# A graph layer on one core: SyncE fetches a chunk's 128 rows in 14 turns instead of 16

## The reference

```
xn  = layernorm(x)
x   = x + gnn(xn, src, dst) + mix(xn)        # gnn: two SAGE layers, mix: linear attention + MLP
x   = x + ffn(layernorm(x))                  # each row goes to one of 8 experts

sage(x) = (segment_sum(x[src], dst) / max(count, 1)) @ Wl.T + b + x @ Wr.T
gnn     = sage2(relu(sage1(xn)))
```

## Time and profile before

| | |
|---|---|
| runs before | 2389.92, 2390.24, 2394.78 us; median 2390.24 us |
| profiled execution | 2393.41 us, of it a span of 2391.6 us |
| PE busy | 1915.2 us (80%) |
| POOL busy | 1650.4 us (69%) |
| DVE busy | 1152.5 us (48%) |
| ACT busy | 549.1 us (23%) |
| gathers L758 | 771 of layer 1 (737.5 us busy), 771 of layer 2 (731.2 us busy) |
| DMA engines | busy 35.4% with GpSimd's queue, 4.4% and 7.0% with the other two |

### The profile page before, as it was taken

The page is one execution under the profiler, slowest core; times in us unless marked ns, Lnnn a source line. Parts: engine busy times, 40 slices in busy tenths (PEclk is TensorE's granted clock), DMA queues, the critical chain, the costliest instruction groups (busy, mean ns, idle before and its releaser), DMA issues.

```text
span 2391.6 us, 54474 instructions
## 1 busy us (share of the span) xinstructions
PE 1915.2 (80%) x9589; PEld 1184.8 (50%) x9590; DVE 1152.5 (48%) x3201; ACT 549.1 (23%) x1242; POOL 1650.4 (69%) x1753
## 2 busy tenths in 40 slices
PE   3799999888688878786899999987665543689999
PEld 2456555555455555552455555443332211378887
DVE  8545554443577777774655545543332221342222
ACT  6434443333122222220122222211110000101111
POOL 6777777777777777757777777777777777164442
PEclk9999999999899999897899999998776655689999
DMA  7444444444444444434455454444444443455552
GB/s 218 137 131 130 133 131 128 128 127 127 134 138 136 129 140 140 143 100 143 150 163 161 153 164 152 152 153 142 129 131 120 117 120 108 149 184 169 166 163 82
DMA packets 166333, 336.14 MB, mean 141 GB/s; under 512 B 41189, under 2 KB 101063, under 8 KB 166181
## 3 DMA queue, kind: packets, MB, share of 16 engines
q0 software_dynamic: 84768, 245.32, 35.4%
q10 hardware_dynamic: 42630, 58.35, 7.0%
q1 hardware_dynamic: 38786, 31.12, 4.4%
HBM read 273.98 MB, written 58.72 MB: 139 GB/s over the span
## 4 chain that ended last, share of the span: by engine, by line
PE 40%; POOL 24%; issue 14%; DVE 11%; DMA 3%; DVEq 3%; ACT 1%; POOLq 1%; ACTq 1%; SPq 1%
POOL big L758 23%; PE bank L572 14%; PE bank L1790 8%; PE bank L1555 7%; PE bank L1778 2%; PE bank L1561 2%; DMA mbuf<-qT_d 2%; PE bank L1711 1%; DVEq L506 1%; PE bank L1585 1%; PE bank L1580 1%; DVE m_s L1085 1%; POOL big L768 1%; DVE bank L1079 1%; DMA big<-hh_d,edges 1%
## 5 line engine op out<-in xcount | busy, mean ns | idle before, releaser
L758 POOL DMA_INDIRECT big<-xh_d,edges x771 | 737.5, 957 | 245.0 <-issue 227.4
L758 POOL DMA_INDIRECT big<-hh_d,edges x771 | 731.2, 948 | 242.7 <-issue 228.0
L1555 PE MATMUL bank<-big,S 128*128 x1960 | 585.2, 424 | 225.5 <-SPq L629 186.3
L957 DVE SCALAR_TENSOR_TENSOR S<-edges,tv,bank 128x512 f16<-128x512 f32 x490 | 365.5, 747 | 439.8 <-PE bank L1555 253.8
L1555 PEld LDWEIGHTS bank<-big,S 128*128 128x128 f16 x1960 | 203.0, 104 | 511.2 <-issue 368.4
L1553 PE MATMUL bank<-ones,S 128*128 128x1 f16 x980 | 166.0, 169 | 40.7 <-SPq L629 30.6
L572 PE MATMUL bank<-turned,x1T 128*128 128x512 f32 x392 | 195.2, 620 | 0.0
L779 POOL DMA_INDIRECT out_dram<-big,node_s x56 | 56.8, 1014 | 145.5 <-DVE big L1290 136.7
L1483 ACT ACTIVATE x1T<-bank 128x256 f32<-128x256 f32 x49 | 18.8, 383 | 503.9 <-PE bank L1561 494.4
L1553 PEld LDWEIGHTS bank<-ones,S 128*128 128x128 f16 x980 | 95.7, 98 | 54.2 <-SPq L629 37.7
L1290 DVE SCALAR_TENSOR_TENSOR big<-bank,prob_s,res 128x256 f32<-128x256 f32 x56 | 27.1, 484 | 180.1 <-PE bank L1792 180.1
(11 more groups left out here) (229 smaller groups left out, 2903.6 us busy)
## 6 DMA issues: line engine op xcount, KB each, us to landing
hx_d<-mbuf ACTq DMA_DIRECT2D x49, 512.0 KB
big<-xh_d,edges POOLq DMA_INDIRECT x771
big<-hh_d,edges POOLq DMA_INDIRECT x771
st<-xh_d SPq DMA_DIRECT2D x768, 1.0 KB
ik<-hh_d SPq DMA_DIRECT2D x768, 1.0 KB
ik<-xh_d SPq DMA_DIRECT2D x640, 1.0 KB
st<-hh_d SPq DMA_DIRECT2D x640, 1.0 KB
big<-in_fwd_dram SPq DMA_DIRECT2D x8, 1024.0 KB, 12.3
```

Source lines behind the costliest of these rows:

```text
L758: e.indirect_dma_start(GS[layer][:, r, n % SC, :], None, table, bass.IndirectOffsetOnAxis(ap=srcx[:, n:n + 1], axis=0)).then_inc(d_g[r], 16)
L957: VI.done(e.scalar_tensor_tensor(S[:, walk.u, :, :], dst[:, bass.ds(c * SC, SC)].unsqueeze(2).to_broadcast([P, SC, P]), tv[:, bass.ds(k, 1 ...
L1555: ins = e.matmul(AGG[:], S[:, walk.u, j, :], GS[layer][:, bass.ds(slot, 1), j, :].rearrange("p a c -> p (a c)"), start=False, stop=False, ...
```

## The change

`SP_TURNS` goes from 16 to 14, and `SP_SPLIT` says which rows a turn takes: nine, in the 7th and 14th turn ten. A block is then 15 superchunks long; SyncE's chunks are those of superchunks 15, 30, ... 195, 13 in each layer instead of 11, and GpSimd issues 769 gathers in each layer instead of 771. Only superchunk 196 lies behind the last placement.

```
-SP_ROWS = 8
-SP_TURNS = P // SP_ROWS
+SP_TURNS = 14
+SP_SPLIT = [P // 2 * n // (SP_TURNS // 2) for n in range(SP_TURNS)] + [P]
+assert SP_SPLIT[SP_TURNS // 2] == P // 2
 SP_CHUNKS = (SUPER - 1) // (SP_TURNS + 1)
...
                 _, of = nc.values_load_multi_w_load_instructions(
-                    row_src[:, turn * SP_ROWS:(turn + 1) * SP_ROWS], engines=[mybir.EngineType.SP], min_val=0, max_val=N - 1,
+                    row_src[:, SP_SPLIT[turn]:SP_SPLIT[turn + 1]], engines=[mybir.EngineType.SP], min_val=0, max_val=N - 1,
                     skip_runtime_bounds_check_because="a source node of an edge")
-                for p, row in enumerate(of, turn * SP_ROWS):
+                for p, row in enumerate(of, SP_SPLIT[turn]):
```

## The result

The changed kernel takes 2719.35 us (median of 5 runs, 2717.19 to 2719.63) against 2390.24 us; the ratio is 1.137, 95% interval 1.1356 to 1.1380. The prediction was 2386.5 us, 2383 to 2392. It missed by 333 us and in sign. The profiled execution took 2717.19 us, its span is 2715.3 us.

A forecast was written before the change was run, and what follows sets the result against it. GpSimd's gathers were taken to bound layer 2 and layer 1 up to superchunk 108, then part B. Savings of 2.50 and 1.25 us, all else 0, sum to -3.75: from 2390.24 to 2386.5 us, range 2383.0 to 2392.0.

The forecast's parts named there:

- What bounds the kernel now: GpSimd's gathers bound layer 2 and layer 1 up to superchunk 108; part B bounds layer 1 after that.
- steps 1 and 2: Gathers spared: two in layer 2, -2.50 us; in layer 1 one counts before part B, -1.25 us.
- Only layer 2 saves: Rival: the 1.25 us earlier start is lost in layer 1's part B; 2387.7 us, chance 17%.
- Step 3: SyncE's longer turns: nine rows 4.53 us, ten 4.94, under a superchunk's 5.00; 2.5 us spare per block, cost 0.
- two estimates of 71.2 and 70.5: SyncE's block time in us against GpSimd's 73.75: 70.5 summed from its parts, 71.2 from its waits for landings.
- The rival on SyncE's lateness: Layer 2's last relays come late if a SyncE block exceeds 72.85 us; at 74.25, 2399.9 us; chance 8%.
- Step 4: Start of layer 2: SyncE, 11.9 us behind, makes up 2.5 in each block, over five blocks; cost 0 at the end.
- Step 5: Last placement moves from superchunk 187 to 195, its copy hidden under the gathers; cost 0, at most 1.5 us, still hidden.
- Step 6: 512 more row DMAs and four more copies beside part B; cost taken as 0, within -0.5 to +0.5 us.
- the rival on the queries' loads: Part B's 49 query waits, 1.1 us each, grow with the number of rows: +9.7 us, 2396.2 us, chance 5%.

The follow-up runs named there:

- the reads of sixteen: The changed kernel with its own turns of nine and ten rows, but row numbers read 16 at a time from words 0, 16, 32: 2391.94 us, ratio 0.9990.
- The split in fours: The changed kernel with its 14 turns split 8, 8, 12, 8, 8, 12, 8 rows in each half: 2393.2 us, ratio 1.0006.
- both kernels with cheap reads: The changed kernel split 8, 8, 12, 8, 8, 12, 8 rows, ratio 1.0006, and with row numbers read 16 at a time, ratio 0.9990.

## Why the prediction was wrong

**What bounds the kernel now, and steps 1 and 2** had the places right. With the reads of sixteen, layer 2 gives back 2.4 of the 2.50 us. The 1.25 of layer 1 did not arrive at the end of part B in that kernel. In the seven profiles of kernels at about 2390 us part B's first load of queries starts between 621.15 and 623.47, and from there to layer 2's first gather it takes 450.7 to 455.0 us. Both vary by more than the 1.25, and whether such a gain counts can't be told from these. *Only layer 2 saves*, given 17%, is what that kernel showed: forecast a gain of 2.5, measured 1.9 us between the medians, with an interval from 0.2 to 4.5.

**Step 3 is where the prediction failed**, in the sentence "Nine rows make it 4.53, ten 4.94". It priced only the added row DMAs at 0.41 us, took the rest of the turn (4.12 - 8 x 0.41 = 0.84) as fixed, and took the sum of the block from that. The DMAs were right. The rest, nearly all the read of the row numbers, was not fixed: it depended on how many words it reads and on which word it starts at, and the change touches just these two. In 10 of 14 turns the read went from 0.69 to 2.06 or 2.26 us, in the other four from 0.69 to 0.94. With the medians of the 14 turns a block's reads cost 25.3 us, where 14 reads of 0.69 and 0.3 more in each of the two turns behind the fetch of row numbers would be 10.3. That puts 15.0 us on the forecast 71.2 and makes 86.2; the blocks take 85.8 in layer 1 and 87.8 in layer 2. Over 13 blocks that is (85.8 - 73.75) x 13 = 157 us in layer 1, where 138.8 were measured, since the kernel before was over GpSimd's pace there too: 976.8 us up to the relay of superchunk 195, where its 767 gathers at 1.253 us come to 961. In layer 2 it is (87.8 - 73.75) x 13 = 183, where 185.2 were measured. No row of the trace of before shows a read that isn't eight words from an aligned word, so it was an operation that the trace did not show, and step 3 gave it no bounds from both sides. Its two estimates of 71.2 and 70.5 agreed because both carried the same assumption.

**The rival on SyncE's lateness** had the place, the sign and the threshold (72.85 us in a block), but a price for 74.25. It had 8% and should have had a second case, since over GpSimd's 73.75 each us comes back in up to 26 blocks of both layers once the ring is full, and not only in the last relays of layer 2.

**Step 4** was mis-sized too. The change was to make 2.5 us up in each block. The split in fours, whose reads cost some 11.3 us in a block, about one more than the forecast, never caught up in layer 2: its relays came 14.9 us behind the last gather's end at superchunk 4, 17.8 at 124 and still 10.5 at 194, where a relay in step comes 1.8 behind. The spare of a block was nothing in the first half of the layer and some 1.5 us in the second, not 2.5 throughout. From the relay of superchunk 15 to that of 195 its blocks took 73.6 us on the mean, 3.1 over step 3's first sum of 70.5. As an estimate, 1.1 to 1.8 of that are the reads and 1.1 are pauses that the turn at 1092.11 doesn't contain: some 0.35 us once in 128 instructions, and a block has 417. The second estimate, 71.2, took all of SyncE's waiting for landings as spare; but a SyncE that is late still waits for its own copies, 11.2 us in the 390 us after 1110 against 2.0 in the kernel before. Why the first half is dearer (its reads took some 13 us in a block, later 11.6) stays open. That GpSimd doesn't feel it was right: none of its waits for TensorE in layer 2 is over 0.3 us.

**Step 5** was right in the kernel of sixteen-word reads: the relay, at 2041.58, follows the last gather's start at 2038.86 by 2.7 us, its own landing. **Step 6**, 512 more row DMAs at 0, fits both kernels with cheap reads: 1.0006 (0.9996 to 1.0015) and 0.9990 (0.9981 to 0.9999). Their upper ends, even with the forecast saving of 3.75 added, leave the rows 7.3 and 3.5 us at most, so the rival on the queries' loads at 9.7 us falls; that they cost nothing at all is not shown. That rival's wait of 1.1 us was too low besides: over the whole run it was 70.9 us for 49 loads, 1.45 each.

## What to carry to other kernels

When a change alters the size or the first element of an access, every instruction that takes this access has a new price, also the one that looks like fixed overhead; if the trace has it in one form only, its price is open and needs bounds from both sides. When a sequencer's work is paced against another engine with 3% to spare, ask first what one of its instructions would cost in another form, since each us over the margin comes back in every block. SyncE's register reads from SBUF should start at a multiple of four words and take many words at once, as the reads here show for up to 16. A saving of 2 to 4 us in 2390 can't be judged from one profile of each kernel: first see how much the same program varies.

## What the runs showed of the hardware that was not expected

A read of 32-bit words from SBUF into SyncE's registers costs by its start. Started off a multiple of 16 bytes it pays about 0.2 us for each word, also for words in whole aligned groups. Started at a multiple it pays 0.24 to 0.31 us for four words, and about 0.2 for each word left over. Medians of 50 to 350 reads each: 0.69 us for 8 words, 0.93 for 12 and 1.24 for 16, aligned; 1.86 for 8, 2.06 for 9 and 2.26 for 10, unaligned.

SyncE also pauses for some 0.35 us each time it has gone through 128 instructions, as at 606.77 in the chain above; that was so in the profiles of all ten kernels.

GpSimd's gathers had two paces in one and the same program, 946 and 949 ns in the median, steps of 1.251 and 1.254 us; over a layer that is some 2 to 3 us. What sets it is not shown.
